# The first stage's row sums: two heads in one product instruction, five accumulated rows folded to three, and a buffer of its own for the middle tiles

## The reference

```python
kv  = einsum('bhil,bhjl->bijhl', k_, v_)            # k = v = ctx
y   = irfft(rfft(kv, 2L) * rfft(ssm_kernel, 2L))[..., :L]
out = y + kv * D
out = einsum('bijhl,bhil->bjhl', out, q_)           # q = layernorm(x)
x   = x + tanh(g_xattn) * out

t       = layernorm(x)
scores  = softmax(t @ gate_w.T); weights, indices = top_k(scores, 2)
y       = sum_e swiglu(t, w1[e], w3[e], w2[e]) * w_e
z       = swiglu(t, sw1, sw3, sw2)                  # shared experts
x       = x + tanh(g_ffn) * (y + z)
```

## Time and profile before

| | |
|---|---|
| median of 3 runs | 746.34 us (744.3 to 748.05) |
| the profiled execution | 744.08 us, of which 742.2 us are its span |
| PE busy | 716.8 us, 97% |
| DVE busy | 569.5 us, 77% |
| ACT busy | 459.6 us, 62% |
| POOL busy | 373.4 us, 50% |
| end of stage one (last conv) | 207.7 us |
| granted TensorE clock | 1.000 |

### The profile page before, as it was taken

The page is one execution under the profiler, slowest core; times in us unless marked ns, Lnnn a source line. Parts: engine busy times, 40 slices in busy tenths (PEclk is TensorE's granted clock), DMA queues, the critical chain, the costliest instruction groups (busy, mean ns, idle before and its releaser), DMA issues.

```text
span 742.2 us, 15553 instructions
## 1 busy us (share of the span) xinstructions
PE 716.8 (97%) x4602; PEld 675.0 (91%) x4602; DVE 569.5 (77%) x1111; ACT 459.6 (62%) x659; POOL 373.4 (50%) x190
## 2 busy tenths in 40 slices
PE   3999999999999999999998999999998999999998
PEld 3999999999989999899998999898998999999997
DVE  7899999898955578428888589848996699679942
ACT  7575757575432322126888488858895789678931
POOL 5998888886401065032454334444644454434420
PEclk9999999999999999999999999999999999999999
DMA  7778787877522122563557588766556664432101
GB/s 234 232 228 278 219 271 225 266 225 244 171 100 44 29 43 43 155 170 78 165 162 203 129 238 263 199 174 165 157 134 204 156 193 101 74 68 49 44 1 57
DMA packets 48404, 114.88 MB, mean 155 GB/s; under 512 B 7472, under 2 KB 8624, under 8 KB 48336
## 3 DMA queue, kind: packets, MB, share of 16 engines
q1 hardware_dynamic: 35792, 89.67, 36.6%
q0 software_dynamic: 12544, 24.40, 17.6%
HBM read 157.78 MB, written 29.26 MB: 252 GB/s over the span
## 4 chain that ended last, share of the span: by engine, by line
PE 68%; DVE 12%; DMA 7%; issue 6%; ACT 3%; SPq 3%; ACTq 0%; DVEq 0%; POOLq 0%
PE pair L1288 19%; PE bank L1288 14%; PE pair L1313 12%; PE pair L1224 8%; PE bank L1313 6%; PE bank L1175 4%; DMA out<-ys,slot_info 3%; PE pair L1296 3%; DMA raw<-in_weights 2%; PE bank L1235 2%; SPq L516 2%; DVE prod L819 2%; DVE x L790 2%; DVE bank L824 2%; DVE rows L831 1%
## 5 line engine op out<-in xcount | busy, mean ns | idle before, releaser
L1140 DVE TENSOR_TENSOR w_lo<-raw,w_hi 128x1408 fp32r<-128x1408 f32 x94 | 148.9, 1622 | 46.5 <-ACT w_hi L723 46.0
L1428 POOL DMA_INDIRECT out<-ys,slot_info x47 | 89.2, 1898 | 115.9 <-DMA out<-ys,slot_info 53.9
L1415 POOL DMA_INDIRECT tn<-t_rows,slot_info x47 | 74.1, 1577 | 118.4 <-DVE tT_lo L878 79.5
L723 ACT ACTIVATE w_hi<-raw 128x1408 fp32r x94 | 125.0, 1374 | 10.1 <-DMA raw<-in_weights 7.8
L1224 PE MATMUL pair<-kv_hi,toep_hi 128*128 128x288 f32 x320 | 100.6, 314 | 1.3 <-DMA toep_lo<-kpad_lo 1.3
L1224 PE MATMUL pair<-kv_lo,toep_hi 128*128 128x288 f32 x320 | 95.3, 298 | 0.0
L1224 PE MATMUL pair<-kv_hi,toep_lo 128*128 128x288 f32 x320 | 95.1, 297 | 0.0
L1145 DVE TENSOR_TENSOR w_lo<-raw,w_hi 128x1536 fp32r<-128x1536 f32 x47 | 82.4, 1753 | 10.3 <-ACT w_hi L730 10.3
L1366 POOL TENSOR_TENSOR kv_lo<-kv,kv_hi 128x2304 fp32r<-128x2304 f32 x15 | 77.3, 5151 | 6.0 <-ACT kv_hi L619 6.0
L730 ACT ACTIVATE w_hi<-raw 128x1536 fp32r x47 | 69.3, 1475 | 7.4 <-DMA raw<-in_weights 7.4
L819 DVE TENSOR_TENSOR prod<-pair,q 128x256 f32<-128x256 f32 x128 | 53.5, 418 | 14.8 <-PE pair L1224 9.2
(11 more groups left out here) (221 smaller groups left out, 1978.2 us busy)
## 6 DMA issues: line engine op xcount, KB each, us to landing
raw<-in_weights SPq DMA_DIRECT2D x94, 704.0 KB
raw<-in_weights SPq DMA_DIRECT2D x47, 768.0 KB
toep_hi<-kpad_hi SPq DMA_DIRECT2D x15, 512.0 KB, 4.6
toep_lo<-kpad_lo SPq DMA_DIRECT2D x15, 512.0 KB, 6.2
cx<-in_ctx SPq DMA_DIRECT2D x15, 384.0 KB, 6.3
stage<-in_weights SPq DMA_DIRECT2D x16, 272.0 KB, 6.7
xt<-in_x SPq DMA_DIRECT2D x16, 256.0 KB, 6.4
xr<-in_x SPq DMA_DIRECT2D x16, 256.0 KB, 6.7
```

The source lines that it names most:

```text
L723: act.activation(w_hi[s % 2][:, a:b], raw[:, bass.ds(half + a, b - a)], ACT.Copy).then_inc(hi_ok[n_], 1)
L1140: dve.tensor_tensor(w_lo[s % 2][:, a:b], raw[:, bass.ds(half + a, b - a)], w_hi[s % 2][:, a:b].bitcast(F32), ALU.subtract).then_inc(lo_ok[ ...
L1415: pool.indirect_dma_start(out=tn[o % 2][:], out_offset=None, in_=t_rows, in_offset=bass.IndirectOffsetOnAxis(ap=slot_info[:, 3 * i:3 * i + ...
L1428: pool.indirect_dma_start(out=out, out_offset=bass.IndirectOffsetOnAxis(ap=rows, axis=0), in_=ys[o % 2][:], in_offset=None, bounds_check=R ...
```

## The change

1. **Order of rows in a tile.** The rows of a tile are now (head, channel, batch) instead of (channel, head, batch). The host's transposes of x and of the output follow, and `q_copy` writes q so that one head's columns lie together. The two ACT instructions have as many elements as before.
2. **`products`.** Both heads are done by one instruction: multiplies of 384, 128 and 512 elements (six instructions become three, `PROD_STEPS` 6 to 3), the same add of 512, and a new add of 256 that folds the four `rows` to two. The first multiply waits for the convolution of both heads. The fold waits for the add by a new semaphore `added_rows`.
3. **`sum_rows`.** Three transposes instead of five.
4. **Units 0 to 2.** Unit 1 writes its hidden values to banks 5 and 3 and no longer waits for unit 0's; unit 2 waits for unit 0's only. `turn_t` of tile 15 moves into the middle of up(1).
5. **The middle tiles' rows.** The four own tiles between routed ones (`MID`) are loaded into `tn_mid`, the first as soon as the routed units start, each other once the one before is done, and no longer into `tn[o % 2]`. `load_next` for piece C is issued from another place in SP's program, and all weight loads now stand ahead of `load_rows` of a unit.

```diff
-PROD_STEPS = 6
+PROD_STEPS = 3
+SUMROWS = 2
+MID = [o for o, (routed, i) in enumerate(ORDER) if not routed and LEAD <= o < FINAL[0]]
...
+            if n == 1:
+                return [bank[5], bank[3]]
             return ps_h[1 if n >= FREE_H and n % 2 else 0]
...
             for n in range(N_UNITS + 3):
-                u = unit(n)
-                for o in fills_at(n):
-                    load_rows(o)
...
-                if u and u.routed and u.i + 1 < SLOT_TILES - 1:
-                    load_next(u.i + 1, (0, 1))
-                if u and u.routed and 2 <= u.i:
-                    load_next(u.i - 1, (2,))
+                if (s := split_up_at(n)) is not None and s + 1 < SLOT_TILES - 1:
+                    load_next(s + 1, (0, 1))
+                if (s := split_down_at(n)) is not None and s + 1 < SLOT_TILES - 1:
+                    load_next(s + 1, (2,))
+                for o in fills_at(n):
+                    load_rows(o)
+                for k, o in enumerate(MID):
+                    if n == (FIRST_R if k == 0 else last_unit(MID[k - 1]) + 1):
+                        wait(sp, tTl_ok, MID[k - 1] + 1 if k else 0)
+                        sp.dma_start(tn_mid[:], tT_t[ORDER[o][1]]).then_inc(tn_mid_in, 16)
...
-                for h in range(2):
-                    y = ps_conv[par][:, h * 512:h * 512 + 512]
...
-                    wait(dve, conv_ok, t * 8 + 2 * lb + h + 1)
-                    dve.tensor_tensor(view(pp, po, [[P + G, 4], [G, HD], [1, BATCH]]),
...
-                    dve.tensor_tensor(view(ps_rows, po, [[P, 3], [G, HD], [1, BATCH]]),
...
-                    dve.tensor_tensor(view(ps_rows, po + 3 * P, [[4 * G, 2], [G, 4], [1, BATCH]]),
...
+                wait(dve, conv_ok, t * 8 + 2 * lb + 2)
+                dve.tensor_tensor(view(w, BATCH, [[n, 2], [HB + BATCH, 3], [1, HB]]),
...
+                dve.tensor_tensor(view(w, 2 * n, [[HB, 2], [HB // 2, 2], [1, HB // 2]]),
...
+                wait(dve, added_rows, t * 4 + lb)
+                dve.tensor_tensor(view(ps_rows, 0, [[HB, 2], [P, 4], [1, HB]]),
...
                 wait(dve, prod_ok, (t * 4 + lb + 1) * PROD_STEPS)
-                dve.tensor_tensor(rows[par][:], ps_rows, prod[par][:, 0:L], ALU.add).then_inc(rows_ok, 1)
+                dve.tensor_tensor(rows[par][:], ps_rows, view(w, 0, [[HB, 4], [n, 2], [1, HB]]),
+                                  ALU.add).then_inc(added_rows, 1)
+                wait(dve, added_rows, t * 4 + lb + 1)
+                dve.tensor_tensor(rows[par][:, 0:SUMROWS * P], rows[par][:, 0:SUMROWS * P],
+                                  rows[par][:, SUMROWS * P:], ALU.add).then_inc(rows_ok, 1)
...
-                for r in range(PRODROWS):
-                    part = (rows if r < BLOCKS else prod)[lb % 2]
-                    mm = pe.matmul(ps_o[:, lb * P:(lb + 1) * P], part[:, r * P:(r + 1) * P], ident[:],
-                                   is_transpose=True, start=(r == 0), stop=(r == PRODROWS - 1))
+                for r in range(SUMROWS + 1):
+                    part = rows[lb % 2][:, r * P:(r + 1) * P] if r < SUMROWS else last
...
-                wait(pe, hid_ok, n if n <= FREE_H else n - 1)
+                if n == 1:
+                    pe.wait_ge(q_ok, 2 * TILES)
+                else:
+                    wait(pe, hid_ok, n if 2 < n <= FREE_H else n - 1)
...
+                    if n == 1 and c == 2:
+                        turn_t(At(TILES - 1))
...
-                if n == 0:
-                    turn_t(At(TILES - 1))
```

More of the change, by code:

```diff
@@ L224, in program @@
         tn = sb2("tn", [P, L])
+        tn_mid = sb("tn_mid", [P, L])
         tT_hi = sb2("tT_hi", [P, L], F32R)
@@ L353, in tn_count @@
         def tn_count(o):
-            return 16 * sum(ORDER[k][0] == ORDER[o][0] for k in range(o % 2, o + 1, 2))
+            return 16 * sum(ORDER[k][0] == ORDER[o][0] and k not in MID for k in range(o % 2, o + 1, 2))
         def last_unit(o):
@@ L496, in load_rows @@
                 routed, j = ORDER[o]
-                if not routed:
+                if not routed and o not in MID:
                     wait(sp, tTl_ok, o - 1)
@@ L601, in q_copy @@
                 wait(act, q_turned, t + 1)
[L602 to L605, removed]
+                act.activation(view(q[p][:], 0, [[2 * GW, BLOCKS], [GW, 2], [1, HB]]),
+                               view(ps_q, 0, [[P, BLOCKS], [HB, 2], [1, HB]]), ACT.Copy).then_inc(q_ok, 1)
+                act.activation(view(q[p][:], HB, [[2 * GW, BLOCKS], [GW, 2], [1, HB // 2]]),
+                               view(ps_q, 0, [[P, BLOCKS], [HB, 2], [1, HB // 2]]), ACT.Copy).then_inc(q_ok, 1)
             def tT_copy(t):
@@ L691, in tile_hi @@
                     src = ps_t
+                elif o in MID:
+                    act.wait_ge(tn_mid_in, 16 * (MID.index(o) + 1))
+                    act.wait_ge(up_ok, last_unit(o - 2) + 1)
+                    src = tn_mid
                 else:
@@ L830, in products @@
-                wait(dve, prod_ok, (t * 4 + lb + 1) * PROD_STEPS)
-                dve.tensor_tensor(rows[par][:], ps_rows, prod[par][:, 0:L], ALU.add).then_inc(rows_ok, 1)
+                y, z, w = ps_conv[par][:], q[t.odd][:], prod[par][:]
+                qo, n = lb * 2 * GW, 4 * HB
+                wait(dve, summed, t * 4 + lb - 1)
+                if lb == 0:
+                    wait(dve, q_ok, (t + 1) * 2)
+                wait(dve, conv_ok, t * 8 + 2 * lb + 2)
+                dve.tensor_tensor(view(w, BATCH, [[n, 2], [HB + BATCH, 3], [1, HB]]),
+                                  view(y, HB, [[512, 2], [HB, 3], [1, HB]]),
+                                  view(z, qo, [[GW, 2], [0, 3], [1, HB]]), ALU.mult).then_inc(prod_ok, 1)
@@ new lines, in products @@
+                dve.tensor_tensor(view(w, 2 * n, [[HB, 2], [HB // 2, 2], [1, HB // 2]]),
+                                  view(y, 4 * HB, [[512, 2], [0, 2], [1, HB // 2]]),
+                                  view(z, qo + HB // 2, [[GW, 2], [HB // 2, 2], [1, HB // 2]]),
+                                  ALU.mult).then_inc(prod_ok, 1)
+                wait(dve, added_rows, t * 4 + lb)
+                dve.tensor_tensor(view(ps_rows, 0, [[HB, 2], [P, 4], [1, HB]]),
+                                  view(y, 0, [[512, 2], [HB, 4], [1, HB]]),
+                                  view(z, qo, [[GW, 2], [BATCH, 4], [1, HB]]), ALU.mult).then_inc(prod_ok, 1)
@@ L876, in tile_lo @@
                 dve.wait_ge(tTh_ok, o + 1)
-                src = ps_t if ORDER[o][0] else tn[o % 2]
+                src = ps_t if ORDER[o][0] else tn_mid if o in MID else tn[o % 2]
                 dve.tensor_tensor(tT_lo[o % 2][:], src[:], tT_hi[o % 2][:].bitcast(F32),
@@ L1232, in sum_rows @@
                 wait(pe, rows_ok, t * 4 + lb + 1)
-                for r in range(PRODROWS):
-                    part = (rows if r < BLOCKS else prod)[lb % 2]
-                    mm = pe.matmul(ps_o[:, lb * P:(lb + 1) * P], part[:, r * P:(r + 1) * P], ident[:],
-                                   is_transpose=True, start=(r == 0), stop=(r == PRODROWS - 1))
+                last = prod[lb % 2][:, 8 * HB:]
+                for r in range(SUMROWS + 1):
+                    part = rows[lb % 2][:, r * P:(r + 1) * P] if r < SUMROWS else last
+                    mm = pe.matmul(ps_o[:, lb * P:(lb + 1) * P], part, ident[:],
+                                   is_transpose=True, start=(r == 0), stop=(r == SUMROWS))
                 mm.then_inc(summed, 1)
```

23 lines of the change are left out of this document (4 added, 19 removed).

## The result

The changed kernel takes **811.62 us** (median of 6 runs, 801.64 to 814.76); the kernel before took 746.77 in the same runs (6, 744.3 to 748.41). The ratio is **1.0784**, interval 1.0746 to 1.0821; it leaves out the three slower runs of the changed kernel (814.19 to 814.76, the profiled one among them), which lie over 1.5% above its fastest, so it is smaller than the quotient of the two medians. The forecast had the sign and missed the size by nine tenths: +6.65 us forecast, +59 measured by the ratio and +65 by the medians, far outside 743 to 760. The profiled execution took 814.76 (span 813.0).

A forecast was written before the change was run, and what follows sets the result against it. PE and DVE were taken to be in series in stage one's loop, PE to bound stage two. Terms +11.9 - 0.5 - 1.15 - 3.6 = +6.65 us took the median from 746.34 to 753.0 us; range 743 to 760.

The forecast's parts named there:

- the fold of 256 elements 0.335: DVE's products block: the new fold adds 0.335 us to a block of 2.45 us, 0.25 more than before.
- ACT's and POOL's work in a tile stays hidden: Stage one: this work is shorter than the tile, which becomes longer, so it adds no time.
- I take 2.45, since every piece has a near row: DVE's new products block: 2.45 us chosen between bounds of 2.20 and 2.60, against 2.20 before.
- the range's 2.60: DVE's products block: upper bound if each wait in it costs another 0.05 us; total 760 us, chance 0.12.
- The loop of 13.01 us: Stage one, per tile: 12.22 + 0.52 + 0.25 + 0.24 - 0.22 = 13.01 us, PE then waiting for DVE.
- +11.9: Stage one: 0.79 us more a tile over 15 tiles, +11.9 us in all.
- The start, -0.5: Tile 0: two sum_rows before conv(0,3) lose two transposes each at PE's slow first pace, -0.5 us.
- Waiting for both heads, +0.52: Products(t,3): DVE starts only after both heads' convolution, so products(t+1,0) starts 0.52 us later.
- The passage, -1.15: Passage to stage two: unit 1's own banks remove waits; up(2) comes at E + 12.9 instead of 14.07, -1.15 us.
- The middle tiles, -3.6: Stage two's middle tiles: with `tn_mid` SP no longer waits and weights come in time, -3.6 us; bounds 0 and 9.65.
- if the loads then meet the scatters earlier: Middle tiles: bound of 0 gain instead of 3.6 us, if earlier loads slow the scatters.
- The one that ended slower (760): Rival, DVE's block: waits cost more than the line says, block 2.60 us, +6.8 us, total 760 us; chance 0.12.

The follow-up runs named there:

- The fold in PSUM: Changed kernel with the add split in two, so the fold reads one input from PSUM and one from SBUF: 764.71 us, ratio 1.0219.
- short GpSimd instructions: Changed kernel, fold untouched, with most of GpSimd's `kv_lo` and `kv` product work left out from tile 2 on: 767.91 us, ratio 1.0268.
- by heads: Changed kernel without the fold (five transposes), products(t,3) alone done head by head: 742.55 us, ratio 0.9929; with `turn_t` one chunk earlier too, 740.54.
- Stage two's part alone: Kernel before plus only unit 1's banks, the `turn_t` place, `tn_mid` and the order of SP's loads: 743.41 us, ratio 0.9931.

## Why the prediction was right and wrong

- **"the fold of 256 elements 0.335", and "ACT's and POOL's work in a tile stays hidden".** This is the step that failed: the fold took 1.28 us in the mean, since it waits while GpSimd works. The duration came from rows of multiplies that read one input from PSUM, and the fold reads both from SBUF; the loop of stage one in the trace of before has no such instruction. Outside the loop that trace had rows for it: `tT_lo` with both inputs in SBUF took 2.55 us beside GpSimd and 0.68 clear of it. The cost of the fold should have been bounded from both sides, with GpSimd's longest instruction, 5 us, as the upper end. "I take 2.45, since every piece has a near row" said the opposite. The unstretched block is indeed 2.46 (141.37 to 143.83), and the range's 2.60 covered only errors of size, no other mechanism. The Trainium skill states the rule on another page than the one I weighed, "SBUF — State Buffer", section "SBUF: two separate sides": VectorE and GpSimd share a port pair, held by one of them for its whole instruction, and a VectorE instruction with two SBUF inputs contends for it with a GpSimd instruction that reads SBUF. The traces agree (5.13 us against 5.04 of `kv_lo`, and 0.42 with one input in PSUM). By it the first question to a new DVE instruction would have been where its inputs lie.
- **What it cost.** The fold in PSUM ends stage one at 225.95 and the changed kernel at 278.56. These 52.6 us are about what the stretched folds lose (54.9, some of it off the path) and the 12 us that PE runs at the lower clock after its waits; the profiles don't divide them further. No term of the sum had PE's clock in it. The earlier trace rows show 1.00 for a PE that hardly waits; the longer waits brought 0.86.
- **The loop of 13.01 us.** The mechanism was right, the size a little low, but it carries only some 16 to 18 of the 70.7 us; most of the loss has another cause than the one that gave the forecast its sign. With short GpSimd instructions a tile takes 13.26 in the mean (39.99 to 225.65 for 14 tiles, by the start of conv(t,3)), PE is busy for 87% of that time, and it waits 0.79 us in front of sum_rows(t,1) where about 1 was forecast. Products(t,3) starts 0.02 after the convolution as forecast; but products(t+1,0) starts 2.84 after it and not 2.49, with an idle time of 0.28 put down to "issue" that the old order had not shown. In the version with a split add a tile takes 13.41, its block being longer. For 15 tiles that is 4 to 6 us more than +11.9.
- **The start, -0.5.** Not seen. Tile 0's last convolution ended at 24.33 before, and at 24.7, 25.1 and 23.9 in the versions with a split add, without a fold, and by heads: -0.5 to +0.8. Stage two's part alone, with the old stage one, shows 23.8, so one profile can't tell a term of 0.5.
- **Waiting for both heads, +0.52.** Its place was right in versions with a fold. Without one it costs nothing, since PE is the bound at 12.13 us a tile. Here my reading of before was one-sided: PE and DVE were in series at 12.22, but PE's own work was 12.13 (12.25 and 12.16 from tile 1 on). The two bounds lay within 0.1 us of each other: relief for DVE alone could bring no more than that, and relief for PE that lengthens DVE's blocks lengthens the loop.
- **The passage, -1.15.** Failed where I wrote that `turn_t` "waits for nothing": what mattered was who waits for `turn_t`. A store, a load and the next tile's split hang on it, and with it 0.87 later up(3) starts only 0.17 earlier, although up(2) comes 12.2 us after the last convolution, earlier than the 12.9 forecast. In the changed kernel even up(2) comes 14.5 after it: up(0) takes 5.49 us there, at a granted clock of 0.69 between 281.90 and 287.40, where 3.95 was forecast; PE had waited 0.45 and 0.46 us shortly before, and no run separates what lowered the clock there.
- **The middle tiles, -3.6.** The wait for `w_lo` shrank as forecast, but waits for scatters grew. That bound had been named ("if the loads then meet the scatters earlier"). By the ratio stage two's part gives -5.2 against -4.75 forecast; in single profiles nothing of it is seen.
- **The rivals.** The one that ended slower (760) had the waits inside the block as its mechanism; none had GpSimd. The rule of the Trainium skill that I did weigh ("VectorE: DVE Perf Modes", section on the TRN2 errata: a fixed part for each instruction) said that DVE would lose nothing; by its formula the old block is 2.70 us, not the 2.67 that I wrote, and the new one 2.65. The unstretched block of 2.46 is 0.26 longer than the old one of 2.20, so here the measurement decides against it.

## What to carry to other kernels

Before adding an elementwise instruction to DVE, ask where its inputs lie: with both in SBUF it can wait for an elementwise instruction that GpSimd is running, and then its cost is up to GpSimd's longest such instruction, not its own. If a value comes out of PSUM anyway, leave one operand there: one instruction more made this kernel over 40 us faster. And an operation that has no row in the loop under study is looked for in the rest of the old trace, beside the engines that it could meet; failing that its bounds come from the longest thing that it could meet, not from its nearest relative in size.

## What the runs showed of the hardware

- A DVE add of 128x256 with both inputs in SBUF takes 0.42 us, or until 0.28 to 0.29 us after the end of the GpSimd instruction beside it: 5.13 beside one of 5.04, 0.59 beside one of 0.32. With one input in PSUM it took 0.42 every time (64 of 64). A split of 512 elements (0.69 alone) ended 0.55 after GpSimd's. In both sizes the held instruction ends its own duration less 0.14 us after GpSimd is done.
- GpSimd's gathers and scatters (DMA_INDIRECT) did not hold such instructions. In the kernel before, 108 of the 141 `w_lo` splits of stage two, with both inputs in SBUF, ran beside one and none was stretched; the larger group (durations in ns, shortest, median and longest):

```profile
L1140 DVE TENSOR_TENSOR w_lo<-raw,w_hi x94: 1606/1621/1699, 333.8 to 701.0; 128x1408 fp32r<-128x1408 f32 x94
```

- The wait goes both ways: a GpSimd instruction of 64 columns that began together with a fold took 0.61 us in place of 0.32, in the version with short GpSimd instructions.
- DVE's multiply with one input and its output in PSUM ran beside GpSimd without loss: 0.69 us for 512 elements (42 of 64 met one).
- After a wait of 5.33 us PE's matmuls of 288 columns started 0.24 us apart for some 4.5 us, at a granted clock of 0.50, then 0.13 apart at 1.00. Waits of 0.6 to 0.8 us in the loop of the version with short GpSimd instructions left the clock at 1.00 (43.2 to 228.8).
